# A gated cross-attention network on one core: copies of q and k first on ScalarE, tokens and keys a unit sooner, maximum and subtraction ahead of the sum on VectorE

## What is computed

```python
def _L0_xattn_ref(x, context, Wq, Wk, Wv, Wo, bo):      # _L1_xattn_ref: the same with 16 heads
    q = (x @ Wq).reshape(B, S, HEADS, DIM_HEAD).transpose(0, 2, 1, 3)
    k = (context @ Wk).reshape(B, L, HEADS, DIM_HEAD).transpose(0, 2, 1, 3)
    v = (context @ Wv).reshape(B, L, HEADS, DIM_HEAD).transpose(0, 2, 1, 3)
    attn = jax.nn.softmax(jnp.einsum('bhsd,bhld->bhsl', q, k) * scale, axis=-1)
    out = jnp.einsum('bhsl,bhld->bhsd', attn, v)
    return out.transpose(0, 2, 1, 3).reshape(B, S, INNER) @ Wo + bo
...
x = x + jnp.tanh(g_xattn[0]) * _L0_xattn_ref(_layernorm(x, axis=-1), ctx_768, ...)
x = x + jnp.tanh(g_ffn[0]) * _L0_ffn_ref(_layernorm(x, axis=-1), ...)
x = x + jnp.tanh(g_xattn[1]) * _L1_xattn_ref(_layernorm(x, axis=-1), ctx_768, ...)
x = x + jnp.tanh(g_ffn[1]) * _L1_ffn_ref(_layernorm(x, axis=-1), ...)
```

## Time and profile before

| | us |
|---|---|
| median of 3 runs (2034.89 to 2048.37) | 2038.03 |
| the profiled execution | 2044.66 |
| its span in the trace | 2042.9 |
| first attention, first to last maximum on DVE | 30.8 to 357.8 |
| second attention, first to last maximum on DVE | 1366.4 to 1905.9 |

### The profile page before, as it was taken

The page is one execution under the profiler, slowest core; times in us unless marked ns, Lnnn a source line. Parts: engine busy times, 40 slices in busy tenths (PEclk is TensorE's granted clock), DMA queues, the critical chain, the costliest instruction groups (busy, mean ns, idle before and its releaser), DMA issues. The chain is left out here.

```text
span 2042.9 us, 95028 instructions
## 1 busy us (share of the span) xinstructions
PE 1785.4 (87%) x39513; PEld 1389.3 (68%) x39513; DVE 1554.4 (76%) x3645; ACT 1553.0 (76%) x2637; POOL 671.9 (33%) x921
## 2 busy tenths in 40 slices
PE   3788888788799999999999999967888888888798
PEld 3777777534366666666666666757777777777687
DVE  4788887579688888888888888765777777777654
ACT  3687877466699999999999998856777777777443
POOL 3677777442000000000000000014555555555465
PEclk8899999799799999999999999988999999999799
DMA  6755555379200000000000001005665555555233
GB/s 158 146 114 112 119 113 113 101 270 372 71 13 14 12 14 12 14 12 14 12 14 12 14 12 52 2 24 118 150 156 139 137 141 139 138 146 142 68 114 114
DMA packets 371233, 185.79 MB, mean 91 GB/s; under 512 B 290366, under 2 KB 350822, under 8 KB 371046
## 3 DMA queue, kind: packets, MB, share of 16 engines
q1 hardware_dynamic: 370198, 182.55, 34.4%
q10 hardware_dynamic: 848, 0.71, 0.1%
HBM read 68.95 MB, written 42.86 MB: 55 GB/s over the span
## 5 line engine op out<-in xcount | busy, mean ns | idle before, releaser
L1646 DVE TENSOR_TENSOR h<-g,h 128x1024 f16<-128x1024 f32 x256 | 313.4, 1224 | 137.9 <-ACT h L1571 137.6
L245 PEld LDWEIGHTS psE<-ew,h 128*128 128x128 f16 x6144 | 350.9, 98 | 56.0 <-issue 40.1
L245 PE MATMUL psE<-ew,h 128*128 128x128 f16 x6144 | 365.0, 219 | 12.8 <-DVE eo L1656 6.0
L1566 ACT ACTIVATE g<-psH,eb1T 128x512 f32<-128x512 f32 x512 | 330.3, 680 | 30.5 <-PE psH L245 24.1
L723 POOL TENSOR_TENSOR Ph<-E,Ph 128x512 f16<-128x512 f32 x192 | 222.4, 1159 | 304.1 <-ACT Ph L640 304.1
L1586 POOL TENSOR_TENSOR shared<-shared 128x128 f16<-128x128 f32 x1 | 0.4, 428 | 846.6 <-ACTq L1387 846.6
L1571 ACT ACTIVATE h<-g 128x1024 f16<-128x1024 f32 x256 | 270.6, 1057 | 8.1
L704 POOL TENSOR_TENSOR E<-E,rden 128x512 f32<-128x512 f32 x192 | 200.0, 1042 | 51.2 <-DVE rden L753 50.6
L562 PE MATMUL psQK<-shared 128*64 128x128 f16 x3072 | 114.6, 226 | 76.6 <-DMA shared<-shared 71.6
L245 PE MATMUL psH<-shared,ew 128*128 128x512 f16 x768 | 178.6, 383 | 0.0
L245 PE MATMUL psH<-xg,ew 128*128 128x512 f16 x768 | 176.9, 380 | 0.0
(11 more groups left out here) (284 smaller groups left out, 3810.9 us busy)
## 6 DMA issues: line engine op xcount, KB each, us to landing
keys_ahead<-shared SPq DMA_DIRECT2D x64, 512.0 KB, 4.9
shared<-keys_ahead SPq DMA_DIRECT2D x64, 512.0 KB, 3.8
rawe<-in_L_ffn_w_dram SPq DMA_DIRECT2D x32, 256.0 KB, 3.1
wb<-rw SPq DMA_DIRECT2D x64, 128.0 KB, 2.0
rows<-places SPq DMA_DIRECT2D x110, 64.0 KB, 2.6
out_dram<-x SPq DMA_DIRECT2D x7, 512.0 KB, 3.2
context_T<-shared SPq DMA_DIRECT2D x64, 48.0 KB, 2.4
PT<-Ph SPq DMA_TRANSPOSE x192, 3.4
```

What stands on the lines that cost most here:

```text
L245: last = e.matmul(to, a, b, start=start and n == 0, stop=stop and n == 2, **flags)
L1566: e.activation(g32[:, ft, :], psH[:, ft, :], ACT.Gelu_apprx_tanh, bias=b1T[:, a.expert(1) * FT + ft:a.expert(1) * FT + ft + 1]).then_inc(s ...
L1646: e.tensor_tensor(h[:, 1 - par, 1, 2 * q:2 * q + 2, :], g32[:, 2 * q:2 * q + 2, :], h[:, 1 - par, 0, 2 * q:2 * q + 2, :], ALU.subtract)\
```

## The change

In words: (1) ScalarE copies both parts of q and k of the first attention one behind the other, ahead of the copy of v and of exp. (2) The normalised tokens are made for the unit four ahead instead of three. Their high float16 part moves from ScalarE to VectorE, for the unit four ahead, and the low part is made for the unit three ahead instead of two. (3) On SP the transposition of tokens stands first in the body, the keys come for the unit two ahead, and the context stands behind the transposition of `Ph`. (4) VectorE's maximum and subtraction of j-1 stand ahead of the sum and reciprocal of j-2. (5) Starts of the loops and, between VectorE's bodies, the last two stages of the norm's root follow.

```diff
@@ sync
-                        a, a2, nx, soon = (Unit(j, k) for k in (0, 2, -1, -2))
+                        a, a2, soon = (Unit(j, k) for k in (0, 2, -2))
+                        if soon.opens and (first or soon.j.off > 0):
+                            transpose_tokens(e, soon)
...
-                        if nx.opens and not first and nx.j.off > 0:
-                            load_keys(e, nx)
-                            load_context(e, nx)
+                        if soon.opens and not first:
+                            load_keys(e, soon)
                         if a2.on:
                             wait(e, s["plo"], a2.j)
...
-                        if soon.opens and (first or soon.j.off > 0):
-                            transpose_tokens(e, soon)
+                        nx = Unit(j, -1)
+                        if nx.opens and not first and nx.j.off > 0:
+                            load_context(e, nx)
@@ scalar
-                        a, a1, a2, a5, later = (Unit(j, k) for k in (0, 1, 2, 5, -3))
+                        a, a1, a2, a5, later = (Unit(j, k) for k in (0, 1, 2, 5, -4))
...
                             projected(0)
+                            if first:
+                                projected(1)
...
-                        if a.on and first:
-                            projected(1)
...
                             e.activation(xn[:, later.tp, :], tile_of(later.t, x), ACT.Identity, bias=column_of(later.t, nmr),
                                          scale=column_of(later.t, rstd)).then_inc(s["ln"], 1)
-                            on_slot(e, "xc", later, -1)
-                            wait(e, s["ln"], later.t)
-                            copy(parted[:, later.slot, 0, :], xn[:, later.tp, :]).then_inc(s["xh"], 1)
@@ gpsimd
-                        a, a2, soon = (Unit(j, k) for k in (0, 2, -2))
+                        a, a2, soon = (Unit(j, k) for k in (0, 2, -3))
@@ vector
-                        a, a1, a2, a5, soon, later = (Unit(j, k) for k in (0, 1, 2, 5, -2, -3))
+                        a, a1, a2, a5, soon, later = (Unit(j, k) for k in (0, 1, 2, 5, -3, -4))
 
-                        if a2.on:
-                            wait(e, s["exp"], a2.j)
-                            wait(e, s["mul"], a2.j - 2)
-                            e.tensor_reduce(den[:, a2.par, :], E[:, a2.four], AX.X, ALU.add).then_inc(s["den"], 1)
-                            wait(e, s["den"], a2.j)
-                            e.reciprocal(rden[:, a2.par, :], den[:, a2.par, :]).then_inc(s["rden"], 1)
                         if a1.on:
...
                         if a2.on:
+                            wait(e, s["exp"], a2.j)
+                            wait(e, s["mul"], a2.j - 2)
+                            e.tensor_reduce(den[:, a2.par, :], E[:, a2.four], AX.X, ALU.add).then_inc(s["den"], 1)
+                            wait(e, s["den"], a2.j)
+                            e.reciprocal(rden[:, a2.par, :], den[:, a2.par, :]).then_inc(s["rden"], 1)
...
+                        if later.opens and (first or later.j.reg is not None or later.j.off > 0):
+                            wait(e, s["ln"], later.t)
+                            on_slot(e, "xc", later, -1)
+                            e.tensor_copy(parted[:, later.slot, 0, :], xn[:, later.tp, :]).then_inc(s["xh"], 1)
                         if first and later.on:
-                            on_slot(e, "xc", later, -1)
                             e.tensor_copy(parted[:, later.slot, 2, 0:DC], tile_of(later.t, ctx32)).then_inc(s["chi"], 1)
```

More of the change, by code:

```diff
@@ L685, in _ @@
                             e.wait_ge(s["nmr"], part + 1)
-                            pipeline(e, body, lo - 3, hi - 3, max(lo - 3, 8), hi - 3, 4)
-                        for j in range(U - 3, U + 5):
+                            pipeline(e, body, lo - 4, hi - 4, max(lo - 4, 8), hi - 4, 4)
+                        for j in range(U - 4, U + 5):
                             body(Step(None, 0, j))
                     else:
-                        for name in ("ln", "xh"):
-                            e.sem_inc(s[name], 1)
-                        pipeline(e, body, -1, U, 8, U - 3, 4)
+                        e.sem_inc(s["ln"], 1)
+                        pipeline(e, body, -2, U, 8, U - 4, 4)
                         for j in range(U, U + 5):
@@ L735, in _ @@
                     if first:
-                        pipeline(e, body, -2, U + 2, 8, U - 2, 4)
+                        pipeline(e, body, -3, U + 2, 8, U - 3, 4)
                     else:
@@ L763, in body @@
                         if a2.on:
+                            wait(e, s["exp"], a2.j)
[3 more added lines that the diff above has]
+                            e.reciprocal(rden[:, a2.par, :], den[:, a2.par, :]).then_inc(s["rden"], 1)
+                        if a2.on:
                             wait(e, s["vh"], a2.j)
@@ L800, in _ @@
                         e.wait_ge(s["c0"], 16)
-                        for j in range(-3, 0):
+                        for j in range(-4, 0):
                             body(Step(None, 0, j))
@@ L820, in _ @@
                                 body(Step(None, 0, j), (24,) if j < 40 else ())
-                                for stage in ((0, 1), (2,), (3,), (4,), (5,), ())[j - lo]:
+                                for stage in ((0, 1), (2,), (3,), (4, 5), (), ())[j - lo]:
                                     norm(part, slice(lo + 8, lo + 24), stage)
@@ L836, in _ @@
                         queue_shift(e, s, 0, late, nmr)
-                        e.sem_inc(s["xl"], 1)
-                        pipeline(e, body, -1, U, 8, U - 3, 4)
+                        for name in ("xh", "xl"):
+                            e.sem_inc(s[name], 1)
+                        pipeline(e, body, -2, U, 8, U - 4, 4)
                         pa, pb = psQK[:, 1, :], psS[:, 0, :]
```

## The result

The changed kernel takes 2198.11 us in the median of 4 runs (2195.89 to 2198.52), the kernel before 2042.15 us (4 runs). The ratio is 1.0763, 95% interval 1.072 to 1.0805: it is slower by 7.6%. The forecast was 2191 us in a range of 2063 to 2245. The profiled execution has a span of 2196.7 us, 153.8 us more than before; the first attention takes 417.9 us from first to last maximum (327.0 before), the second 596.9 us (539.5), and what lies between them 1013.4 us (1008.6).

The account below looks back on a forecast made before the run. Bound before: PE waiting, on the SyncE queue ring (second attention) and ScalarE's second copy of q and k (first). Terms 58 + 88 + 7 = 153 us on 2044.66 give 2198, median 6.6 lower: 2191 us, range 2063 to 2245.

Parts of the forecast that it names:

- The ring through SyncE's queue: Second attention before: projection, `Ph`'s transposition, tokens' transposition queued behind it, next projection; sets the pair's 8.3 us.
- the second copy of q and k: First attention before: ScalarE's copy, behind exp, keeps PE's scores waiting 0.66 us a unit; without it about 4.3 us.
- DVE's ring: Both attentions after: reciprocal, GpSimd's product, ScalarE's `Ph` and tokens, DVE's cast; pair 9.36 us, unit 6.7; 75 in 100.
- The ring through `ln`: After the change, DVE's cast of the tokens waits for `ln`, which waits through `Ph` and `mul` for DVE's own reciprocal.
- The hold: GpSimd's running instruction blocks DVE's cast until it is done: pair 9.36 us with it, 8.23 without.
- the rival without a hold: GpSimd does not block DVE's cast: +25 us in all, 2063 us; 11 in 100.
- The sum: Second attention +58 us, first attention +88, its first 13 units +7: 153 us on the profiled 2044.66, so 2198; median 2191.
- The sub-turn of the weights: First attention, GpSimd's 1.16 us subtraction: DVE's cast slips in before `plo`; unit 7.04 us, or 6.85 if not put back.
- Where TensorE waits: After the change, PE's waits for the tokens' DMA and `psQK` copy go; its scores wait for DVE's subtraction instead.
- the faster rival: Both waits go, DVE does not stand on `ln`, PE becomes the bound: 101 us gained, 1937 us; 4 in 100.
- a clock under 0.95: Sign that the forecast is wrong: PE's granted clock below this in the steady stretches, 1.00 before.
- The third rival: PE's clock falls too, 0.5 us a pair and 0.3 a unit: +28 + 15, 2234 us; 6 in 100.

Follow-up runs that it names:

- e10: e5 with the tokens' transposition behind that of `Ph` on SyncE again, as in the kernel before: 2027.99 us, ratio 0.9928.
- e5: e1 with VectorE's sum and reciprocal ahead of maximum and subtraction again: 1963.29 us, ratio 0.9626.
- e8: Kernel before with only ScalarE's new order in the first attention, both copies of q and k ahead of v and exp: 2036.33 us, ratio 0.9986.
- e6: e5 with the second copy of q and k of the first attention behind exp again: 1966.34 us, ratio 0.9645.
- e1: Changed kernel with the high part of the tokens again a copy on ScalarE, right behind `ln`: 2000.88 us, ratio 0.9797.
- e7: Changed kernel with ScalarE making the second attention's normalised tokens five units ahead instead of four, the cast staying on VectorE: 2093.61 us, ratio 1.0262.
- e3: Changed kernel with VectorE's casts of tokens and context done as a sum over one element: 2109.61 us, ratio 1.032.
- e9: e5 with the high part of the first attention's context copied on ScalarE instead of cast on VectorE: 1936.86 us, ratio 0.9477.
- e4: Kernel before with only VectorE's new order, maximum and subtraction ahead of the sum: 2065.19 us, ratio 1.0109.

## Why the prediction was right, and where it was not

**What bound the kernel before.** Right for the second attention. The ring through SyncE's queue returns with its 8.28 us a pair when that one step is undone (e10), and TensorE's own work, put at 7.1 us a pair, is what remains when nothing else holds it (7.24 in e5). Wrong for the first. It said that the second copy of q and k made TensorE wait, and that without it the unit would fall towards 4.3 us; alone that copy's move gives 4.88 (e8), and in e5 it is worth 3 us in all (e6). The error did not reach the sum, because there DVE's ring, longer than either, sets the time. What held the first attention of the kernel before stays open.

**The ring through `ln`.** Right in each step: the cast sits idle with ScalarE's tokens as releaser, `Ph` waits for the product in every unit. Shown twice, by opening the ring on either side of the cast (e1, e7).

**The hold.** Right, and it was the term with the widest bounds, 9.36 against 8.23 us a pair. e3 shows it: 0.846 against 0.286 us for the same elements. The fall of 0.52 us a pair is close to that difference of 0.56. So the rival without a hold (2063 us) is out.

**The sum.** First attention: +90.9 us measured from first to last maximum, +95 forecast (88 in the steady part and 7 in the units before it). Measured, the 51 intervals took 332.8 us where 340 was worked out: 47 with the cast at 6.76 us, the norm's instructions among them, and four without it at 3.8 us, where five at 4.94 had been put. The units before, 30.3 to 115.4, took 10 us more than in the kernel before; they are 12 intervals, and the forecast counted 13. Second: +57.4 measured, +58 forecast, but by two misses that cancel, which is luck. The pair takes 9.49 us and not 9.36: the even units take 6.02 and 6.13 us in turn where 5.98 was worked out, the odd ones 3.42 where 3.38 was. Inside the even unit two more misses nearly cancel: ScalarE starts `Ph` 0.12 us behind the product (1781.09 to 1781.21) and not 0.04 as in the earlier trace rows, and the cast ends 0.08 us behind `plo` and not 0.15. In all that is 7 us more over 56 pairs, and the ends of the stretch, left as they were in the sum, gave 8 us back. Another 4.8 us lie between the attentions, where the forecast said that nothing would change. The three parts make 153 us, as forecast; the 7 us between 2191 and 2198 are the 6.6 us by which the forecast put the median of the runs below the profiled execution, where the changed kernel's lies 0.3 us below.

**The sub-turn of the weights.** The step said that GpSimd's `plo` might be put back by the cast that slips in before it, 7.04 us, or 6.85 if not. It is not put back: most units with the weights' subtraction take 6.7 us, most of those with the cast of weights 6.5 (6.45 forecast).

**Where TensorE waits.** Wrong in a detail. I had its scores waiting for DVE's subtraction; in the second attention most of its idle time stands ahead of the output projection, for DVE's residual (35.2 us) and ScalarE's copy of `psO` (32.3), and 8.2 us ahead of the scores. In the first, from 120 to 430 us, it is DVE's residual again:

```profile
PE psY L592 <- DVE x L779: 68.8, 42, 2.2
```

All of these hang on the same ring, so the time is the same.

**The removed waits.** The forecast priced their removal in the faster rival only, at 1937 us. With both rings open and nothing else moved the time is 1963 us (e5): the unit stays at 4.85 us, and e9 shows that VectorE's held cast of the context is part of what keeps it there, a bound that the rival did not name. That e9 comes out at 1937 is in part luck, since its unit takes 4.44 us and its pair 7.24, where the rival had 4.3 and 7.1.

**The clock.** The prediction named a clock under 0.95 in the steady stretches as a sign that it was wrong, and this sign came: 0.93 in the mean of the first attention. The third rival was right that it would fall and that DVE's ring would hide most of it; the 0.3 us a unit that it priced did not come through. Two windows of the changed kernel:

```profile
215.00:240.00 25.00, 17.83 (x557) 16.12 (x561) 21.34 (x50) 13.91 (x26) 12.64 (x18) 0.84 0.44 89
...
365.00:390.00 25.00, 16.88 (x612) 14.82 (x614) 20.80 (x39) 13.00 (x26) 13.39 (x19) 1.00 0.44 92
```

At 0.84 three units take 6.47, 6.68 and 6.44 us (from 218.22), at 1.00 three take 6.59, 6.71 and 6.48 (from 366.76): the lower clock cost nothing that one can see, the unit is what DVE's ring makes it. In the second attention the clock stayed at 1.00 with TensorE at 80%.

## What to carry to other kernels

When a step is moved to another engine, ask in which order that engine's own earlier result reaches it again: a wait for the last instruction of a neighbour's body is a full round trip if the neighbour's body waits for you. Take the producer one body ahead, or leave the step where its producer is. And look at what GpSimd runs at that moment: a VectorE cast or a two-operand instruction on SBUF stands until it is done, so its length in a trace says where it was put, not what it costs.

## What the runs showed of the hardware

- A VectorE cast of 128x128 from float32 to float16 takes 0.23 us alone and 0.8 or 0.9 us beside a 1.15 us GpSimd subtraction in the second attention, and ends 0.07 to 0.10 us behind it. The same copy as a sum over one element takes 0.286 us in the same place. This is the rule of the Trainium skill, "SBUF — State Buffer", section "Who interferes with whom", which exempts the reduction on trn2; the trace agrees, and here it is worth 88 us of a kernel.
- Not expected: an order of VectorE's instructions that waits for nothing new cost 1.1% (e4), with its two held instructions longer by 0.53 us a unit. Why it cost is argued from these rows and not shown.
- Not expected: between two GpSimd instructions back to back, VectorE's waiting cast gets in, and GpSimd's next one is not seen to start later. In the changed kernel, at 282.62:

```profile
281.96 1.15 POOL L718 TENSOR_TENSOR ew<-rawe,ew 128x512 f32 x1
...
282.62 0.58 DVE L773 CAST shared<-xna 128x128 f16<-128x128 f32 x1 [0.94 <-ACT xna L679]
...
283.07 1.15 POOL L721 TENSOR_TENSOR Ph<-E,Ph 128x512 f16<-128x512 f32 x1
283.11 1.17 DVE L775 CAST shared<-ctx 128x96 f16 x1
```

The cast ends at 283.20, 0.09 us behind L718 (283.11), while L721 has started at 283.07; the next cast is held until 284.28, behind L721. In all 24 units of 115 to 448 us in which the cast meets L718, L721 starts 0.03 to 0.04 us ahead of L718's end, as it does behind the weights' cast, and takes its usual 1.14 to 1.16 us.
